# One chunk solve, three sums: keeping the applies in their PSUM bank and splitting the copies over two engines

## The reference

```python
def step(state, inp):
    q_t, k_t, v_t, b_t, d_t = inp
    state = state * d_t[..., None, None]
    Sk = jnp.einsum('bhi,bhij->bhj', k_t, state)
    delta = (v_t - Sk) * b_t[..., None]
    state = state + jnp.einsum('bhi,bhj->bhij', k_t, delta)
    o = jnp.einsum('bhi,bhij->bhj', q_t, state)
    return (state, o)
...
y = o * jax.nn.silu(zz)
y = y * jax.lax.rsqrt(jnp.mean(y * y, axis=-1, keepdims=True) + 1e-06) * norm_w
out = jnp.einsum('btv,ov->bto', y.reshape(B, T, VDIM), W_out)
```

## Time and profile before

| | us |
|---|---|
| runs | 1975.21, 1980.0, 1981.11; median 1980.0 |
| the profiled execution | 1971.39 |
| its span | 1969.4 |
| mean granted TensorE clock | 0.971 of full |
| busy: PE, DVE, ACT, POOL | 1749.0, 1519.3, 1226.4, 636.4 |

### The profile page before, as it was taken

How to read it: one execution, slowest core, us unless ns; L and a number is a source line. 1 busy time by engine, 2 the same in 40 slices (tenths; PEclk the granted TensorE clock), 3 DMA queues, 4 the chain that set the end, 5 groups by cost and what they waited for, 6 DMA issues and landing times.

```text
span 1969.4 us, 35372 instructions
## 1 busy us (share of the span) xinstructions
PE 1749.0 (89%) x12824; PEld 1303.0 (66%) x12824; DVE 1519.3 (77%) x2421; ACT 1226.4 (62%) x2155; POOL 636.4 (32%) x442
## 2 busy tenths in 40 slices
PE   7899999999899778889888889888988888988976
PEld 5667676767657566667766667666776666756665
DVE  8788888888674787887777878778777787877853
ACT  3253534444355567777677877768767786777862
POOL 2212222231230535336053261432605326144140
PEclk9999999999999899999999999999999999999988
DMA  3011110101032001101101011010110101101000
GB/s 131 32 62 38 54 61 31 61 31 62 3 99 65 17 16 39 33 23 33 56 23 33 23 34 55 23 34 23 33 55 23 33 23 34 55 23 33 7 1 22
DMA packets 51465, 75.66 MB, mean 38 GB/s; under 512 B 3392, under 2 KB 41792, under 8 KB 51184
## 3 DMA queue, kind: packets, MB, share of 16 engines
q1 hardware_dynamic: 51312, 73.55, 11.7%
HBM read 72.29 MB, written 1.25 MB: 37 GB/s over the span
## 4 chain that ended last, share of the span: by engine, by line
PE 39%; DVE 12%; ACT 10%; issue 9%; POOL 2%; ACTq 0%; DVEq 0%; POOLq 0%
PE bank L897 6%; PE bank L731 6%; PE bank L852 5%; PE bank L742 4%; DVE d_sil L1311 4%; PE bank L790 2%; DVE d_Rb L1377 2%; PE bank L800 2%; PE bank L764 2%; POOL d_dec L1629 2%; DVE d_W L1385 2%; PE bank L873 1%; PE bank L875 1%; PE bank L874 1%; ACT d_TT L1149 1%
## 5 line engine op out<-in xcount | busy, mean ns | idle before, releaser
L1311 DVE SCALAR_TENSOR_TENSOR d_sil<-d_pre,d_w,d_sil 128x1024 f32<-128x1024 f32 x192 | 298.1, 1553 | 5.9 <-ACT d_pre L1081 5.6
L1635 POOL TENSOR_TENSOR d_Rb<-d_V,d_ones 128x512 bf16<-128x512 f32 x32 | 48.0, 1511 | 711.0 <-ACT d_V L1110 711.0
L1363 DVE CAST_PREDICATED d_X<-tables_sb,bank 128x512 bf16<-128x512 int32 x192 | 134.3, 700 | 147.6 <-PE bank L790 146.9
L731 PE MATMUL bank<-xnT,d_w 128*128 128x512 f32 x480 | 244.1, 644 | 0.8
L189 PE MATMUL bank<-xnT,a_w 128*128 128x512 f32 x512 | 237.0, 597 | 0.0
L1145 ACT ACTIVATE d_T<-bank 128x512 bf16<-128x512 f32 x160 | 98.5, 616 | 107.4 <-PE bank L800 105.1
L1629 POOL TENSOR_TENSOR d_dec<-d_dec,d_qk 128x384 f32<-128x384 f32 x128 | 133.2, 1064 | 44.2 <-DVE d_N L1344 44.2
L852 PEld LDWEIGHTS bank<-d_W,d_N 128*128 128x128 f32 x1024 | 122.7, 193 | 35.0 <-DVE d_W L1385 22.4
L189 PEld LDWEIGHTS bank<-xnT,a_w 128*128 128x128 f32 x512 | 90.9, 192 | 78.5 <-issue 78.5
L731 PEld LDWEIGHTS bank<-xnT,d_w 128*128 128x128 f32 x480 | 89.2, 202 | 79.3 <-issue 79.3
L489 POOL TENSOR_TENSOR a_hidc<-a_hid,a_comb 128x512 f32<-128x512 f32 x32 | 44.4, 1387 | 295.0 <-DVE a_hid L336 295.0
(11 more groups left out here) (211 smaller groups left out, 4497.9 us busy)
## 6 DMA issues: line engine op xcount, KB each, us to landing
d_dec<-decay_scratch SPq DMA_DIRECT2D x32, 512.0 KB, 5.7
a_w<-w SPq DMA_DIRECT2D x16, 897.0 KB, 4.6
d_w<-w SPq DMA_DIRECT2D x16, 776.0 KB, 4.8
a_comb<-comb_scratch SPq DMA_DIRECT2D x16, 512.0 KB, 5.5
d_dec<-decay_scratch SPq DMA_DIRECT2D x32, 256.0 KB, 6.0
d_wo<-w SPq DMA_DIRECT2D x16, 256.0 KB, 3.0
f_w<-w SPq DMA_DIRECT2D x8, 256.0 KB, 3.7
tables_sb<-tables SPq DMA_DIRECT2D x1, 1056.0 KB, 8.4
```

The lines of the kernel that those rows point to most:

```text
L731: last = pe.matmul(psum[bank][:, :], cols(slot, (c * KT + k) * P, P), xnT[:, k, h * HALF:(h + 1) * HALF], start=(k == 0), stop=(k == KT - 1))
L1311: dve.scalar_tensor_tensor(sil[c][:, :, :], pre[c % 2][:, :, tap:tap + S], cols(slot, OC + 4 * c + tap, 1), sil[c][:, :, :], ALU.mult, ALU ...
L1363: dve.copy_predicated(left(Xp[lv][:, v], lv), mask.unsqueeze(1).broadcast_to([P, 8, 64]).rearrange("p n (g w) -> p n g w", w=lv), psum[4 + ...
```

## The change

The applies of one chunk accumulate in the bank: only the first matmul of a = 0 has `start=True`, so that after apply a the bank holds the whole W. An update is now a plain copy of the bank into `Wv`: on ACT for value head 0 (`next_w`, new), on DVE for value head 1 (`update`). wup_done becomes two semaphores, wup_done0 and wup_done1. DVE executes four copies a head where it executed eight adds; ACT gets four copies a head. `next_w(i, c, a)` waits for apply a of value head 0, and stands in ACT's queue at four places: after square(0), after the first decays, after the third decays and ahead of `tanh_in(3)`, and after the last decays, ahead of `rnorm(0)`.

```diff
                 for b in range(B):
                     last = pe.matmul(psum[4 + 2 * v][:, b * P:(b + 1) * P], TT[v][:, 2 * b + c, :], Rb[v][:, b, :],
-                                     start=True, stop=True)
+                                     start=(a == 0 and b == 0), stop=(a == 2), skip_group_check=True)
                 last.then_inc(s["apply_ready"], 1)
...
             def residual(i, v, c, a):
...
-                    pe.wait_ge(s["wup_done"], i * 8 + 4 * c + 2 * (a - 1) + v + 1)
+                    pe.wait_ge(s[f"wup_done{v}"], i * 4 + 2 * c + a)
...
             def link(i, v):
-                pe.wait_ge(s["wup_done"], i * 8 + 2 + v + 1)
+                pe.wait_ge(s[f"wup_done{v}"], i * 4 + 2)
...
             def outputs(i, slot, v, h):
-                pe.wait_ge(s["wup_done"], i * 8 + 6 + v + 1)
+                pe.wait_ge(s[f"wup_done{v}"], i * 4 + 4)
...
+            def next_w(i, c, a):
+                act.wait_ge(s["apply_ready"], i * 12 + 6 * c + 2 * a + 1)
+                act.activation(Wv[0][:, :, c, :], psum[4][:, :].rearrange("p (b d) -> p b d", b=B),
+                               ACT.Copy).then_inc(s["wup_done0"], 1)
...
                 if nxt:
                     conv_in(ns, ni, 3)
                     square(ni, 0)
+                next_w(i, 0, 1)
+                if nxt:
                     square(ni, 1)
                     batch_decays(ni, ns, 0)
+                next_w(i, 0, 2)
+                if nxt:
                     tanh_in(ni, 2)
                     batch_decays(ni, ns, 1)
                 for v in range(2):
...
                     first_w(i, v, 1)
                 if nxt:
                     batch_decays(ni, ns, 2)
+                next_w(i, 1, 1)
+                if nxt:
                     tanh_in(ni, 3)
                     batch_decays(ni, ns, 3)
+                next_w(i, 1, 2)
+                if nxt:
                     rnorm(ni, 0)
                     rnorm(ni, 1)
...
-            def update(i, v, c, a):
-                dve.wait_ge(s["apply_ready"], i * 12 + 6 * c + 2 * a + v + 1)
-                if a == 2:
-                    dve.wait_ge(s["wup_done"], i * 8 + 4 * c + v + 1)
-                ww = Wv[v][:, :, c, :]
-                dve.tensor_tensor(ww, ww, psum[4 + 2 * v][:, :].rearrange("p (b d) -> p b d", b=B),
-                                  ALU.add).then_inc(s["wup_done"], 1)
+            def update(i, c, a):
+                dve.wait_ge(s["apply_ready"], i * 12 + 6 * c + 2 * a + 2)
+                dve.tensor_copy(Wv[1][:, :, c, :], psum[6][:, :].rearrange("p (b d) -> p b d", b=B)).then_inc(s["wup_done1"], 1)
...
                         if a:
-                            for v in range(2):
-                                update(i, v, c, a)
+                            update(i, c, a)
```

More of the change, by code:

```diff
@@ L640, in layer1_phase @@
                  "conv_step sil_done max_done kq_done kk_done n_done p_done plain_done tt1_done xp_done sz_done "
-                 "r_done wup_done y_done yss_done yssm_done acc_done col_done mask_done diag_done vb_done ysc_done").split()
+                 "r_done wup_done0 wup_done1 y_done yss_done yssm_done acc_done col_done mask_done diag_done vb_done ysc_done").split()
         s = {n: m.sem(f"d_{n}") for n in names}
```

## The result

The change made the kernel slower: median 1982.6 us against 1976.4 us (20 executions each), ratio 1.003 with a 95% interval of 1.0018 to 1.0043. The forecast was 1971 us, faster, with a range of 1960 to 1981. The profiled execution of after took 1984.3 us (span 1982.4) against 1971.4 (span 1969.4).

A forecast was written before the change was run, and what follows sets the result against it. No engine's share bounds it; the solve's chain of waits does: DVE's updates in chunk 0, PE in chunk 1. Gains 10 x 0.2 + 5 x 1.2 + 0.8 = 8.8 us took 1980.0 to 1971 us, range 1960 to 1981.

The forecast's parts named there:

- Chunk 0, 1.2 us a head: In chunk 0 of the solve DVE leads; two updates of value head 0 leave its queue, 0.60 us each, gaining 1.2 us.
- Chunk 1, nothing: In chunk 1 the chain stands on PE (guard, z projection, residual), so removing DVE updates gains nothing more.
- The tail at straight boundaries: In ten heads followed in straight code, ACT's later table-load tail delays `copy_v`, leaving 0.2 of the 1.2 us.
- The way back: After heads 3, 5, 7, 9 and 11, ACT's return is taken as PE's 2.42 us; the whole 1.2 us stays.
- rival 3: ACT's way back over 3.35 us delays `matrices` five times: 9.2 or 4.2 us slower, 1989 or 1984 us; chance 0.12.
- The clock: TensorE stretches at a granted 0.50, two each loop turn, some 1.7 us each; the sum counted no change in them.
- rival 2: One more half-clock TensorE stretch each turn: 1980 us, chance 0.18; one fewer: 17 us gained, 1963 us, chance 0.08.
- The last head: PE idles 0.20 us before each of four steps behind an update; copies on free ACT gain 0.8 us.
- The starting point: The 8.8 us gain was taken from a median of 1980.0 us, giving 1971.2, say 1971 us.
- the bounds, 0 and 5.96 us: ACT's own way back, hidden in the trace, takes more than nothing and at most 5.96 us.

## Why the prediction was wrong

1. **Chunk 0, 1.2 us a head.** Right: 13.82 to 12.62 us in heads 1 to 14, DVE leading. Head 0 kept nothing of it, and its chunk 1 took 1.3 us longer (13.1 to 14.4 us): its first sixteen residual matmuls on PE (L852, at 719.39) stand behind 4.08 us of idle time and take 3.35 us at a granted 0.58, where before they stood behind 1.80 us and took 2.05 us at 1.00. Three `conv` took 4.58, 4.35 and 4.35 us there before instead of 1.28, and where an add was taken out, the `conv` behind it grew, to 5.16 and 4.92 us. On DVE's timeline and POOL's, after the change, they stand beside POOL's operations of 128x2048:

```profile
700.92 5.16 DVE L1324 SCALAR_TENSOR_TENSOR d_sil<-d_pre,d_w,d_sil 128x1024 f32<-128x1024 f32 x1
706.00 1.27 DVE L1390 TENSOR_TENSOR d_Rb<-d_V,bank 128x512 bf16<-128x512 f32 x2
707.20 4.35 DVE L1324 SCALAR_TENSOR_TENSOR d_sil<-d_pre,d_w,d_sil 128x1024 f32<-128x1024 f32 x1
...
712.07 4.92 DVE L1324 SCALAR_TENSOR_TENSOR d_sil<-d_pre,d_w,d_sil 128x1024 f32<-128x1024 f32 x1
```

```profile
700.48 4.52 POOL L1668 TENSOR_TENSOR x_sb<-x_sb,f_gamma 128x2048 f32<-128x2048 f32 x1 [29.55 <-DVE x_sb L1449]
705.08 5.39 POOL L1670 TENSOR_TENSOR x_sb<-x_sb,f_beta 128x2048 f32<-128x2048 f32 x1
710.54 5.37 POOL L1672 TENSOR_TENSOR acc_sb<-acc_sb,x_sb 128x2048 f32<-128x2048 f32 x1
```

   Each of the three ends 1.08 us after the POOL operation beside it (706.08 and 705.00, 711.55 and 710.47, 716.99 and 715.91), and so it was, within 0.01 us, before the change. Starting a `conv` earlier gains nothing while its end hangs on POOL. DVE's adds with one input in PSUM (L1390) took their usual time beside POOL.

2. **Chunk 1, nothing.** Right: 13.09 us in both, and the z projection's guard leads.
3. **The tail at straight boundaries.** Right in mechanism and nearly in size: `turn_v` to `matrices` grew by 0.83 us; the forecast had 1.0 (1.2 less 0.2 left), so 0.37 us a head was left instead of 0.2. The rows are those described: `unit(0)` behind 3.17 us of waiting for ACT, `copy_v` without idle time.
4. **The way back. This step failed**: "ACT's own way back is hidden in the trace [...] I take PE's 2.42 us, the nearest row: 1468.1, in time. The whole 1.2 us stays." ACT's took 4.2 to 5.7 us, over the 3.35 us from which rival 3 was said to decide, and in the profiled executions the five places took 10.7 us more, where the sum had them unchanged. With the clock out of the way they grew by 18.5 us (45.1 against 26.6), more than all that chunk 0 gained. Idle time of 5.96 us on ACT looked like slack for 3.3 us of work; by the rows after the change 4.2 to 5.7 us of it were ACT's own issue time. And the price of DVE's way back wasn't in rival 3: 4.2 to 4.9 us, begun behind `unit(1)`, which waits for the same tail. It leads only where ACT is unrolled.
5. **The clock.** The sum put it at nothing, and rival 2 gave it in both directions. Both happened: the stretch at 0.50 in `turn_v` after PE's gap went (its saving covered by the wait for ACT), and the inversions of the profiled execution took 8.1 us more (28.9 and 30.0 us in turn where before 27.5 and 29.0 alternate). How much of the 8.1 us is the change and how much the pick of a quick execution of before, one trace of each doesn't tell. It isn't what made the change slower than before: without it the change loses more.
6. **The last head.** 0.8 us forecast; apply to link 0.72 us and link to outputs 0.57 us less, 1.3 us in all. The step was right and its size too small.
7. **The starting point.** The sum began at 1980.0, a median of three executions; over twenty it is 1976.4. The forecast ratio, 0.9956, doesn't hang on it.

Put together at a settled clock: 16.7 us gained in chunk 0 of heads 1 to 14, less 7.4 us at nine straight boundaries and 18.5 us at five ways back, plus 1.1 us from PE's own gaps there, is a loss of 8 us (the traces: 1128.1 against 1120.1); the medians differ by 11.2, the rest lies outside these heads. In the profiled executions as they were, the way back (10.7 us) and the inversions (8.1 us) are what the forecast lacked. Rival 3, given 0.12, is the mechanism that happened, near the bound that the sum had set aside. By its own sum the measured 5.3 us start `copy_v` at 1471.0 and `matrices` at 1474.65, 0.8 us later than before five times: together with the prediction's other terms about 1 us slower. That the median came out 6.3 us slower, between rival 3's two figures of 4.2 and 9.2, is therefore in part the clock, and luck. The choice between the bounds, 0 and 5.96 us, was the whole sign of the forecast at the ways back, and a row of another engine was no measure for it.

The Trainium skill (Runtime: NRT & Kernel Launch, section Instruction fetch mechanics) had said that a taken branch to instructions outside the engine's buffer makes it fetch them before it goes on. The traces agree on three engines: issue time at the way back or a few instructions behind it, PE 1.8 to 2.5 us, DVE 3.0 to 4.9 us where it leads, ACT 4.2 to 5.7 us, each gone where that engine's queue is unrolled. The rows say "issue"; that it is the fetch and no other cost of the loop is argued, as no run tells them apart.

## What to carry to other kernels

Idle time that ends where a loop turns back is not slack until the engine's own time to come back is known: a trace that puts the idle time down to another engine's late data hides it. Before a wait is put into an engine's queue, look at what stands behind it until the next place where others wait for that engine; moving half of the table-load tail ahead of one copy was worth 0.9% here (0.9945 of before against 1.003). And where one of several moved pieces brings nothing by itself (chunk 1's copies), leave it where it was.

## What the runs showed of the hardware

- The way back of a hardware loop costs each engine issue time of its own: PE 1.8 to 2.5 us, ACT 5.3 us on average (4.2 to 5.7), DVE 4.2 to 4.9 us in the change with ACT unrolled, and 3.0 to 3.6 us, inside `matrices`, in the version with copies in chunk 0 only and ACT and PE unrolled. Removing one engine's uncovers the next one's. Straight code for all five engines removed it and showed no price of its own.
- Eight otherwise useless matmuls (some 1.7 us) in an idle stretch of 2.3 us made the kernel before 1.5% faster (0.9853) and its executions agree: 1949.4 to 1952.0 us instead of 1972.4 to 1989.3.
- A bf16 apply that adds to its bank takes no longer than one that overwrites it: 222 ns a matmul in both, and 193.5 us from first apply to link over 14 heads in both. The f32 residuals overwrite in every version, so nothing is shown for them.
- In head 0 `conv` on DVE takes 4.35 to 5.16 us instead of 1.28 while POOL works on 128x2048 tiles (from 700.5 to 715.9 us), and behind that it takes 1.27 us again. Each slow one ends 1.08 us after a POOL operation. That POOL holds it back is argued from these rows alone; no run tried it.
